# Statistics on two engines and begun with the weights, first projection by row pairs, x1 stored from ScalarE's queue

## The chip, the cores and the metric

The kernel runs on one core of a Trainium2 chip. The metric is the device time of one execution in microseconds (us), as a median of several runs. A profiled execution was taken beside them, with a record of every instruction and DMA.

## The reference

Input is x, an image of 512 x 512 positions with 128 channels, in fp32. Two layers follow each other, each as x = x + layer(gn(x)):

```
gn(v)    = (v - mean) / sqrt(var + 1e-5)           # 32 groups of 4 channels, over all positions
layer 0:   a = sigmoid((x@Wa1 + ba1) * (x@Wa2 + ba2))        # 128 -> 16 channels
           b = sigmoid((x@Wb1 + bb1) * (x@Wb2 + bb2))
           z = einsum('ikc,jkc->ijc', a, b)                  # 16 channels
           out = sigmoid(x@Wg + bg) * (layernorm(z)@Wz + bz)
layer 1:   h = (ln(x)@pi) * sigmoid(ln(x)@gi) * mask         # 128 channels, then
           two triangle products of 32 channels each, layernorm, output projection and gate
```

## The kernel before

`pair_layers` builds stages that follow each other behind a barrier of all engines. The weights' preparation (`prepare`), then:

1. `stage1_statistics` reads x once (134 MB) in 16 chunks of 8.4 MB, 128 positions x 128 channels on each of 128 partitions, into a double buffer. VectorE takes a bn_stats (count, mean, variance) of each of the 32 channel groups in every chunk (128 x 512 values each, L286), then aggregates them (L291). TensorE averages over partitions, and both small engines turn the moments into `gn_scale` and `gn_shift`.
2. `stage2_gates` is the first projection. It reads x again, a group of U = 4 image rows (1 MB) at a time, 128 groups. For every row TensorE transposes four 128 x 128 blocks into PSUM (`turn`, L385), ScalarE scales and rounds them to fp16 (`round_high`, L425), VectorE makes the fp16 rest (`rest`, L468). Then `product` (L395) multiplies high and low parts with the 32-wide weights, for m = 0 and m = 1, four rows side by side in the array's columns, 12 matmuls each m. ScalarE adds a bias to m = 0 (`open_first`, L430), VectorE multiplies it with m = 1 (`multiply`, L475), ScalarE takes the sigmoid (`sigmoid`, L436), and SP stores four groups together. The loop's body holds 8 groups and turns 15 times; the last 8 groups are written out.
3. `stage3_triangle` is layer 0's product over k, to z. It is not touched.
4. `stage4_layer0` makes x1, 16 rows a loop turn, 32 turns. For each row i TensorE does the z projection (L793), the gate projection (L795) and the four transposes of row i+4 (L785); ScalarE does the sigmoid (L821) and copies the transposed x (L817); VectorE mixes them (L854) and takes statistics of the sum (L845); GpSimd adds x (L888). The SP queue, per group of 4 rows: wait for the four sums (`added`), store x1 (L754), wait until x's tile is transposed, load x for the group 16 rows on (two DMAs, L745), wait for the z projection, load z (two DMAs, L749).
5. Stages 5 to 7 (mask, projection, triangle products and output of layer 1) are not touched. Stage 7 stores its output from ScalarE's queue (L1602) while SP loads.

The order of the work in each stage is written out by hand in each engine's program. An engine runs its instructions in this order, and each waits for semaphores: `turned`, `rounded`, `rest_ready`, `done` (products), `opened`, `gated`, `sig` in stage 2. A counter that is set ahead (`dve.sem_inc(gated, 2)`) says how many buffers are free at the start.

In stage 2 before, one step of TensorE is: turn rows 0 and 1 of group g+2, product m=0 of group g+1, turn rows 2 and 3, product m=1 of g+1. ScalarE: round rows 0 and 1 of g+2, open g+1, round rows 2 and 3, sigmoid g. VectorE: rest of rows 0 and 1 of g+2, multiply g, rest of rows 2 and 3. `p_ps` is doubled: both products wait for `gated >= g+1`, which multiply(g-2) gives.

Of the kernel before, what the change touches and what calls it, by code (L numbers as in the profile page):

```python
# [11 lines left out]
P = 128  # L12
BANK = 512
# [38 lines left out]
def prepare(nc, K, W):  # L52

    with ExitStack() as stack:
# [31 lines left out]
        with nc.Block() as block:  # L86
            @block.sync
            def _(sp):
                for dst, src in loads:
                    sp.dma_start(dst, src).then_inc(loaded, 16)  # L90
                sp.wait_ge(loaded, 16 * len(loads))
# [162 lines left out]
def stage1_statistics(nc, K, x, N):  # L254

    T = 128
    chunks = N * N // P // T
    x_v = x.rearrange("(p n t) c -> n p t c", p=P, t=T)
    with ExitStack() as stack:
        s = Scope(nc, stack, "s1")  # L260
        xt = s.sbuf("xt", [P, 2, T, P])
        stats = s.sbuf("stats", [P, 32, chunks, 6])
        mv = s.sbuf("mv", [P, 32, 2])
        square = s.sbuf("square", [P, 32])
# [3 lines left out]
        used, aggregated, wide_ready, moments_ready = s.sem("used"), s.sem("aggregated"), s.sem("wide_ready"), s.sem("moments_ready")  # L268
        with nc.Block() as block:
            norm_vector, norm_scalar = norm_from_moments(nc, s, block, K, moments, moments_ready)  # L270

            @block.sync
            def _(sp):
                with sp.Fori(0, chunks // 2) as r:
                    for u in range(2):
                        sp.wait_ge(used, r * 2 + (u + 1))
                        sp.dma_start(xt[:, u, :, :], x_v[bass.ds(r * 2 + u, 1)].rearrange("a p t c -> p (a t) c")).then_inc(loaded[u], 16)

            @block.vector
            def _(dve):  # L280
                dve.sem_inc(used, 2)
                with dve.Fori(0, chunks // 2) as r:
                    for u in range(2):
                        dve.wait_ge(loaded[u], r * 16 + 16)
                        for g in range(32):
# [3 lines left out]
                dve.wait_ge(used, chunks + 2)  # L289
                for g in range(32):  # L290
                    dve.bn_aggr(mv[:, g, :], stats[:, g, :, :].rearrange("p n s -> p (n s)")).then_inc(aggregated, 1)  # L291
                dve.wait_ge(aggregated, 32)
                dve.tensor_tensor(square[:], mv[:, :, 0], mv[:, :, 0], ALU.mult).then_inc(aggregated, 1)
                dve.tensor_copy(wide[:, 0, :, :], mv[:, :, 0:1].to_broadcast([P, 32, 4]))
                dve.wait_ge(aggregated, 33)
                dve.tensor_tensor(square[:], square[:], mv[:, :, 1], ALU.add).then_inc(aggregated, 1)
                dve.wait_ge(aggregated, 34)
                dve.tensor_copy(wide[:, 1, :, :], square[:].rearrange("p (g a) -> p g a", a=1).to_broadcast([P, 32, 4])).then_inc(wide_ready, 1)
# [10 lines left out]
            @block.scalar  # L309
            def _(act):  # L310
                norm_scalar(act)
# [9 lines left out]
def stage2_gates(nc, K, x, ab_d, N):  # L321
# [4 lines left out]
    CB, U, GROUPS = N // P, 4, 8  # L326
    REPS = N // (U * GROUPS)
    x_v = x.rearrange("(i p q) c -> p i q c", q=CB, p=P)
    ab_v = ab_d.rearrange("(g j) c k -> (j c) g k", j=U)
    with ExitStack() as stack:  # L330
        s = Scope(nc, stack, "s2")
        xt = s.sbuf("xt", [P, GROUPS, U, CB, P])
        high, low = s.sbuf("high", [P, 4, U, N], FP16), s.sbuf("low", [P, 4, U, N], FP16)
        first, gate = s.sbuf("first", [P, 2, N]), s.sbuf("gate", [P, 2, N])
        ab = s.sbuf("ab", [P, 2, 4, N])
# [6 lines left out]

        BODY = GROUPS * U

        @block_of(nc)
        def _(block):
            @block.sync
            def _(sp):
                def load(r, k):
                    sp.dma_start(xt[:, k, :, :, :], x_v[:, bass.ds(r * BODY + U * k, U)]).then_inc(loaded[k], 16)  # L350

                def store(r, half):
                    sp.wait_ge(sig, r * GROUPS + (4 * half + 4 + 2))
                    sp.dma_start(ab_v[:, bass.ds(r * GROUPS + 4 * half, 4), :], ab[:, half, :, :]).then_inc(stored[half], 16)
# [5 lines left out]
                with sp.Fori(0, REPS - 1) as r:  # L360
                    for k in range(GROUPS):
                        sp.wait_ge(turned, r * BODY + (U * k + U))
                        load(r + 1, k)
                        if k == 5:
                            store(r, 0)
                    store(r, 1)
                for half in range(2):
                    store(REPS - 1, half)
                for half in range(2):
                    sp.wait_ge(stored[half], REPS * 16 + 16)  # L370

            @block.tensor
            def _(pe):
                for m in range(2):
                    pe.matmul(p_ps[:, m, 0, 0:1], K.Wab4[:, m, :], K.gn_shift[:], start=True, stop=True).then_inc(shifted, 1)
                pe.wait_ge(folded, 2)
                pe.sem_inc(done, 8)

                def turn(r, g, j):

                    if j == 0:
                        pe.wait_ge(loaded[g % GROUPS], (r + g // GROUPS) * 16 + 16)
                    pe.wait_ge(rest_ready, r * BODY + (U * g + j + 1))
                    for q in range(CB):
                        last = pe.transpose(x_ps[:, j, q * P:(q + 1) * P], xt[:, g % GROUPS, j, q, :], K.ident[:])  # L385
                    last.then_inc(turned, 1)

                def product(r, g, m):
                    pe.wait_ge(rest_ready, r * BODY + (U * g + U + U))
                    pe.wait_ge(gated, r * GROUPS + (g + 1))  # L390
                    half = slice(32 * m, 32 * m + 32)
                    for weights, part, start, stop in ((K.Wab_high, high, True, False), (K.Wab_low, high, False, False),
                                                       (K.Wab_high, low, False, True)):
                        for j in range(U):
                            last = pe.matmul(p_ps[32 * j:32 * j + 32, g % 2, m, 0:N], weights[:, half], part[:, g % 4, j, :],  # L395
# [3 lines left out]
                def step(r, g, last=False):  # L399
                    for j in range(U):  # L400
                        if not (last and g + 2 >= GROUPS):
                            turn(r, g + 2, j)
                        if j % 2 == 1 and not (last and g + 1 >= GROUPS):
                            product(r, g + 1, j // 2)

                for g in range(2):
                    for j in range(U):
                        turn(0, g, j)
# [5 lines left out]
                for g in range(GROUPS):  # L414
                    step(REPS - 1, g, last=True)

            @block.scalar
            def _(act):
                act.sem_inc(sig, 2)

                def round_high(r, g, j):
                    act.wait_ge(turned, r * BODY + (U * g + j + 1))
                    if j == 0:
                        act.wait_ge(done, r * (2 * GROUPS) + (2 * g + 2))
                    act.activation(high[:, g % 4, j, :], x_ps[:, j, 0:N], ACT.Copy, scale=K.gn_scale[:]).then_inc(rounded, 1)  # L425

                def open_first(r, g):
                    act.wait_ge(done, r * (2 * GROUPS) + (2 * g + 1 + 8))
                    act.wait_ge(gated, r * GROUPS + (g + 1))
                    act.activation(first[:, g % 2, :], p_ps[:, g % 2, 0, 0:N], ACT.Identity, bias=bias[:, 0:1]).then_inc(opened, 1)  # L430

                def sigmoid(r, g):
                    act.wait_ge(gated, r * GROUPS + (g + 1 + 2))
                    if g % 4 == 0:
                        act.wait_ge(stored[g // 4], r * 16 + 16)
                    act.activation(ab[:, g // 4, g % 4, :], gate[:, g % 2, :], ACT.Sigmoid).then_inc(sig, 1)  # L436

                def step(r, g, last=False):
                    for j in range(U):
                        if not (last and g + 2 >= GROUPS):  # L440
                            round_high(r, g + 2, j)
                        if j == 1 and not (last and g + 1 >= GROUPS):
                            open_first(r, g + 1)
                    sigmoid(r, g)

                for g in range(2):
                    for j in range(U):
                        round_high(0, g, j)
                act.wait_ge(folded, 2)
                open_first(0, 0)  # L450
                with act.Fori(0, REPS - 1) as r:
                    for g in range(GROUPS):
                        step(r, g)
                for g in range(GROUPS):
# [1255 lines left out]
```

## Time and profile before

| | us |
|---|---|
| median of 3 runs | 5023.39 (5017.31 to 5030.55) |
| the profiled execution | 5046.03 |
| its span (first to last instruction) | 5044.3 |

| engine | busy us | share |
|---|---|---|
| TensorE | 4064.9 | 81% |
| VectorE | 4109.2 | 81% |
| ScalarE | 3366.2 | 67% |
| GpSimd | 2717.9 | 54% |

Shares are means over stages with different limits, so they are read by stage. "DMA share" is the mean busy share of the 16 DMA engines; where transfers overlap in an engine it can pass 1. SPq and ACTq are the queues of SyncE and ScalarE as they issue. "x4" behind an instruction says that four alike are merged in a row. An idle time in brackets stands before the instruction, with what ended it.

### The profile page before, as it was taken

The page shows a single profiled execution, that of the slowest core. Times are in us where ns is not written, and L with a number is a line of the kernel's source. Part 1 is how long each engine was busy: PE and PEld are TensorE (multiplying, and loading weights), DVE is VectorE, ACT ScalarE, POOL GpSimd, SP SyncE. Part 2 cuts the span into 40 slices and gives each one's busy share as a digit, 9 for nine tenths or more (in the row PEclk, how much of TensorE's full clock was granted, in tenths as well). Part 3 has the DMA queues.
Part 4 walks back from the last instruction along what each step waited for, and adds up shares of the span by engine and source line. Part 5 has one row for each costly group of instructions (what it writes and reads, how often), then busy time and mean ns, then how long its engine had stood idle before and what let it go on. Part 6 is the DMA issues. An engine that isn't in the chain of part 4 may idle for free. (4 is left out here: it accounts for less than half of the span.)

```text
span 5044.3 us, 90362 instructions
## 1 busy us (share of the span) xinstructions
PE 4064.9 (81%) x26438; PEld 2297.6 (46%) x26438; DVE 4109.2 (81%) x5835; ACT 3366.2 (67%) x4752; POOL 2717.9 (54%) x1426
## 2 busy tenths in 40 slices
PE   0004888893799999879999999989998886888888
PEld 0002555451455555545555555555553333444444
DVE  5888888688788888879999999867778887777777
ACT  0004999754677777658888888746666666888887
POOL 0000000093677777757777777743334435888887
PEclk9999999996899999989999999999999998999999
DMA  6996888653999999968888888776676757999999
GB/s 269 368 373 263 322 321 320 230 175 125 324 355 356 355 354 353 332 234 310 308 309 311 312 309 309 260 254 225 225 238 236 237 195 296 408 406 405 402 403 367
DMA packets 700450, 1532.72 MB, mean 304 GB/s; under 512 B 32800, under 2 KB 50656, under 8 KB 697952
## 3 DMA queue, kind: packets, MB, share of 16 engines
q1 hardware_dynamic: 632800, 1397.68, 78.3%
q10 hardware_dynamic: 67584, 134.23, 6.9%
q8 instruction: 34, 0.56, 0.0%
q14 instruction: 32, 0.26, 0.0%
HBM read 1009.59 MB, written 522.19 MB: 304 GB/s over the span
## 5 line engine op out<-in xcount | busy, mean ns | idle before, releaser
L1634 POOL TENSOR_TENSOR s_oT<-s_gated,s_x1t 128x1024 f32<-128x1024 f32 x256 | 689.6, 2699 | 223.5 <-DVE s_gated L1553 218.5
L888 POOL TENSOR_TENSOR s_x1T<-s_gz,s_xT 128x512 f32<-128x512 f32 x512 | 652.4, 1274 | 202.9 <-DVE s_gz L854 199.8
L1321 PE MATMUL s_y_ps<-s_ab 128*128 128x512 f16 x3072 | 698.0, 385 | 66.3 <-DVE s_ab L1391 64.7
L1026 POOL TENSOR_TENSOR s_low<-s_xc,s_high 128x1024 f16<-128x1024 f32 x256 | 547.8, 2140 | 265.0 <-ACT s_high L989 263.8
L795 PE MATMUL s_g_ps<-s_xT,s_Wg 128*128 128x512 f32 x1024 | 523.7, 593 | 0.0
L634 POOL MEMSET s_total<- 128x2048 f32 x1 | 1.8, 1810 | 960.4 <-POOLq L41 960.4
L854 DVE SCALAR_TENSOR_TENSOR s_gz<-s_z_ps,k_z_bias,s_g 128x512 f32<-128x512 f32 x512 | 384.1, 750 | 164.4 <-ACT s_g L821 162.1
L1321 PEld LDWEIGHTS s_y_ps<-s_ab 128*128 128x128 f16 x3072 | 301.4, 99 | 426.6 <-issue 94.9
L821 ACT ACTIVATE s_g<-s_g_ps,s_bg 128x512 f32<-128x512 f32 x512 | 352.0, 687 | 191.4 <-PE s_g_ps L795 191.4
L1553 DVE SCALAR_TENSOR_TENSOR s_gated<-s_p_ps,k_po_bias,s_gate 128x1024 f32<-128x1024 f32 x256 | 328.6, 1284 | 176.4 <-ACT s_gate L1590 147.7
L1295 POOL TENSOR_TENSOR s_at<-s_at,s_mask 128x1024 f32<-128x1024 f32 x64 | 164.2, 2566 | 502.2 <-DMA s_bt<-h_d 502.2
L468 DVE SCALAR_TENSOR_TENSOR s_low<-s_x_ps,k_gn_scale,s_high 128x512 f16<-128x512 f32 x512 | 359.6, 744 | 88.8 <-ACT s_high L425 88.3
L994 ACT ACTIVATE s_gate<-s_g_ps,k_gi_bias 128x1024 f32<-128x1024 f32 x256 | 284.9, 1113 | 200.3 <-PE s_g_ps L1165 199.8
L785 PEld LDWEIGHTS s_x_ps<-k_ident,s_xt 128*128 128x128 f32 x2048 | 247.5, 142 | 359.9 <-issue 205.3
L1590 ACT ACTIVATE s_gate<-s_g_ps,k_go_bias 128x1024 f32<-128x1024 f32 x256 | 285.8, 1116 | 147.6 <-PE s_g_ps L1499 134.2
L1097 DVE SCALAR_TENSOR_TENSOR s_h<-s_p_ps,k_pi_bias,s_gate 128x1024 f32<-128x1024 f32 x256 | 327.2, 1278 | 63.2 <-DMA h_d<-s_h 26.0
L1064 DVE BATCH_NORM_STATS2 s_stats<-s_x_ps 128x6 f32<-128x256 f32 x1024 | 363.0, 416 | 18.2 <-PE s_x_ps L1142 17.3
L286 DVE BATCH_NORM_STATS2 s_stats<-s_xt 128x512 f32 x512 | 305.5, 682 | 74.8 <-DMA s_xt<-in_x 74.8
L785 PE MATMUL s_x_ps<-k_ident,s_xt 128*128 128x128 f32 x2048 | 315.3, 277 | 54.8 <-DMA s_xt<-in_x 47.7
L845 DVE BATCH_NORM_STATS2 s_stats<-s_x1T 128x512 f32 (+1 forms) x512 | 349.5, 683 | 0.2 <-POOL s_x1T L888 0.2
L817 ACT ACTIVATE s_xT<-s_x_ps 128x512 f32<-128x512 f32 x512 | 302.7, 591 | 51.6 <-PE s_x_ps L785 50.2
L425 ACT ACTIVATE s_high<-s_x_ps,k_gn_scale 128x512 f16<-128x512 f32 x512 | 323.7, 686 | 13.0 <-PE s_x_ps L385 8.3
(215 smaller groups left out, 9695.3 us busy)
## 6 DMA issues: line engine op xcount, KB each, us to landing
s_xt<-in_x SPq DMA_DIRECT2D x128, 1024.0 KB, 6.9
s_xt<-in_x SPq DMA_DIRECT2D x256, 512.0 KB
x_d<-s_x1T SPq DMA_DIRECT2D x128, 1024.0 KB, 8.8
s_xt<-x_d SPq DMA_DIRECT2D x128, 1024.0 KB, 8.7
h_d<-s_h SPq DMA_DIRECT2D x128, 1024.0 KB, 6.4
s_x1t<-x_d SPq DMA_DIRECT2D x128, 1024.0 KB, 13.8
out<-s_ot ACTq DMA_DIRECT2D x128, 1024.0 KB, 9.3
s_mask_b<-mask_d SPq DMA_DIRECT2D x128, 512.0 KB, 4.3
```

Source lines behind the costliest of these rows:

```text
L468: dve.scalar_tensor_tensor(low[:, g % 4, j, :], x_ps[:, j, 0:N], K.gn_scale[:], high[:, g % 4, j, :], ALU.mult, ALU.subtract).then_inc(res ...
L785: last = pe.transpose(x_ps[:, i % 4, q * P:(q + 1) * P], xt[:, i // U, i % U, q, :], K.ident[:])
L795: pe.matmul(g_ps[:, i % 2, 0:N], Wg[:], xT[:, i % 8, :], start=True, stop=True).then_inc(g_prod, 1)
L821: act.activation(g[:, i % 2, :], g_ps[:, i % 2, 0:N], ACT.Sigmoid, bias=bg[:]).then_inc(sig, 1)
L845: dve.bn_stats(stats[:, bass.ds(r * ROWS + i, 1), :].rearrange("p a s -> p (a s)"), x1T[:, i // U, i % U, :]).then_inc(counted, 1)
L854: dve.scalar_tensor_tensor(gz[:, i % 4, :], z_ps[:, i % 2, 0:N], K.z_bias[:], g[:, i % 2, :], ALU.add, ALU.mult).then_inc(mixed, 1)
L888: pool.tensor_tensor(x1T[:, i // U, i % U, :], gz[:, i % 4, :], xT[:, i % 8, :], ALU.add).then_inc(added, 1)
L1026: pool.tensor_tensor(low[:, n % 4, :, :], xc[:, n % 4, :, :], high[:, n % 4, :, :], ALU.subtract).then_inc(rest_ready, 1)
L1064: last = dve.bn_stats(stats[:, row // 16 % 2, row % 16, a, :], x_ps[:, row % 2, 2 * a * P:(2 * a + 2) * P].rearrange("p (e c) -> p c e", c=P))
L1321: last = pe.matmul(y_ps[:, ib, 0:N], ab[:, u % 2, 0, a, kb, ib * P:(ib + 1) * P], ab[:, u % 2, 1, b, kb, :], start=m == 0, stop=m == len(t ...
L1553: dve.scalar_tensor_tensor(gated[:, n % 4, :, :], p_ps[:], K.po_bias[:], gate[:, n % 2, :, :], ALU.add, ALU.mult).then_inc(mixed, 1)
L1634: pool.tensor_tensor(oT[:, n % 4, :, :], gated[:, n % 4, :, :], x1t[:, n // 2, 2 * (n % 2):2 * (n % 2) + 2, :], ALU.add).then_inc(added, 1)
```

## The change

**Statistics.** VectorE keeps 24 of the 32 channel groups; ScalarE takes 8, with two activations a group (Identity and Square), each of which adds up its output in `accum_out`. The first two chunks are issued on the SP queue before the 38 weight loads, in `prepare`. A buffer is loaded again when both engines have read it.

**First projection.** Rounding and rest work on pairs of rows, 1024 elements. `x_ps` has three slots of two PSUM banks each (it had four of one), and `p_ps` one bank for each m (it had two). ScalarE rounds three groups ahead. A loop turn holds 6 groups, 20 turns, and 8 groups are written out. SP reloads six groups, then stores three groups at a time.

**Layer 0's stage.** ScalarE issues the store of x1, at the third row of the next group; SP only loads. The first of the 32 loop turns is written out.

```
 # stage1_statistics
+        def load_ahead(sp):
+            for u in range(2):
+                load(sp, 0, u)
+        prepare(nc, K, W, load_ahead)        # load_ahead(sp) runs ahead of the weights' loads
...
             def _(sp):
+                with sp.Fori(0, chunks // 2 - 1) as r:
                     for u in range(2):
                         sp.wait_ge(used, r * 2 + (u + 1))
+                        sp.wait_ge(summed, r * 2 + (u + 1))
+                        load(sp, r + 1, u)
...
             def _(act):
+                def chunk(r, u):
+                    act.wait_ge(loaded[u], r * 16 + 16)
+                    if not isinstance(r, int) or r or u:
+                        act.wait_ge(summed, r * 2 + u)
+                    for g in range(BY_ACT):
+                        for m, func in enumerate((ACT.Identity, ACT.Square)):
+                            last = act.activation(junk[:, 2 * g + m, :].rearrange("p (t c) -> p t c", c=4),
+                                                  xt[:, u, :, 4 * (BY_DVE + g):4 * (BY_DVE + g) + 4], func,
+                                                  accum_out=sums[:, m, g, bass.ds(r * 2 + u, 1)])
+                    last.then_inc(summed, 1)
...
             def _(dve):     # after 24 bn_aggr
+                dve.wait_ge(summed, chunks)
+                dve.tensor_reduce(total[:], sums[:], AX.X, ALU.add).then_inc(reduced, 1)
+                dve.wait_ge(reduced, 1)
+                dve.tensor_scalar(total[:], total[:], 1.0 / (4 * T * chunks), None, ALU.mult).then_inc(reduced, 1)
+                dve.wait_ge(reduced, 2)
+                for m in range(2):
+                    last = dve.tensor_copy(wide[:, m, BY_DVE:32, :], ...)

 # stage2_gates
-    CB, U, GROUPS = N // P, 4, 8
+    CB, U, GROUPS, SLOTS = N // P, 4, 6, 3
-        x_ps = s.psum("x_ps", [P, U, BANK])
-        p_ps = s.psum("p_ps", [P, 2, 2, BANK])
+        x_ps = s.psum("x_ps", [P, SLOTS, 2, BANK])
+        p_ps = s.psum("p_ps", [P, 2, BANK])
...
             def _(sp):
                 with sp.Fori(0, REPS - 1) as r:
                     for k in range(GROUPS):
+                        reload(r, k)
+                    for half in range(2):
+                        store(r, half)
...
             def _(pe):
+                def turn(r, g, h):
+                    k, n = g % GROUPS, (2 * g + h) % SLOTS
+                    if h == 0:
+                        pe.wait_ge(loaded[k], (r + g // GROUPS) * 16 + 16)
+                    pe.wait_ge(rest_ready, r * PAIRS + (2 * g + h + 1))
+                    for j in range(2):
+                        for q in range(CB):
+                            last = pe.transpose(x_ps[:, n, j, q * P:(q + 1) * P], xt[:, k, 2 * h + j, q, :], K.ident[:])
                     last.then_inc(turned, 1)
                 def product(r, g, m):
-                    pe.wait_ge(gated, r * GROUPS + (g + 1))
+                    pe.wait_ge(rest_ready, r * PAIRS + (2 * g + 2 + SLOTS))
+                    if m == 0:
+                        pe.wait_ge(opened, r * GROUPS + (g + 1))
+                    else:
+                        pe.wait_ge(gated, r * GROUPS + (g + 2))
...
+                def step(r, g, end=None):
+                    for h in range(2):
+                        if end is None or g + 2 < end:
+                            turn(r, g + 2, h)
+                        if end is None or g + 1 < end:
+                            product(r, g + 1, h)
...
             def _(act):
+                def step(r, g, end=None):
                     sigmoid(r, g)
+                    if end is None or g + 3 < end:
+                        round_high(r, g + 3, 0)
+                    if end is None or g + 2 < end:
+                        open_first(r, g + 2)
+                    if end is None or g + 3 < end:
+                        round_high(r, g + 3, 1)
...
             def _(dve):
+                dve.sem_inc(rest_ready, SLOTS)
                 dve.sem_inc(gated, 2)
+                def step(r, g, end=None):
+                    if end is None or g + 2 < end:
+                        rest(r, g + 2, 0)
+                    multiply(r, g)
+                    if end is None or g + 2 < end:
+                        rest(r, g + 2, 1)

 # stage4_layer0
             def _(sp):
-                def group(r, n, last=False):
-                    sp.wait_ge(added, r * ROWS + (U * n + U + 8))
-                    sp.dma_start(x1_d[...], x1T[:, n, :, :]).then_inc(stored[n], 16)
-                    if not last:
+                def group(r, n):
+                    sp.wait_ge(turned, r * ROWS + (U * n + U))
+                    load_x(r + 1, n)
+                    sp.wait_ge(z_prod, r * ROWS + (U * n + U))
+                    load_z(r + 1, n)
...
             def _(act):
+                def store(r, n):
+                    act.wait_ge(added, r * ROWS + (U * n + U + 8))
+                    act.dma_start(x1_d[...], x1T[:, n, :, :]).then_inc(stored[n], 16)
+                def step(r, i, first=False, last=False):
                     act.wait_ge(g_prod, r * ROWS + (i + 1))
                     act.activation(g[:, i % 2, :], g_ps[:, i % 2, 0:N], ACT.Sigmoid, bias=bg[:]).then_inc(sig, 1)
                     if not (last and i + 4 >= ROWS):
                         keep(r, i + 4)
+                    if i % U == 2 and i > U:
+                        store(r, i // U - 1)
+                    elif i % U == 2 and not first:
+                        store(r - 1, GROUPS - 1)
```

## Rows read from the trace of the kernel before

**Rows 1.** Timeline, statistics pass: start us, length us, engine, line, operation, idle time before.

```profile
37.58 1.00 SPq L277 DMA_DIRECT2D s_xt<-in_x  x2
...
62.89 19.09 DVE L286 BATCH_NORM_STATS2 s_stats<-s_xt 128x512 f32 x32 [26.50 <-DMA s_xt<-in_x]
...
83.31 19.09 DVE L286 BATCH_NORM_STATS2 s_stats<-s_xt 128x512 f32 x32 [1.33 <-DMA s_xt<-in_x]
107.59 19.09 DVE L286 BATCH_NORM_STATS2 s_stats<-s_xt 128x512 f32 x32 [5.18 <-DMA s_xt<-in_x]
...
397.57 19.09 DVE L286 BATCH_NORM_STATS2 s_stats<-s_xt 128x512 f32 x32 [0.89 <-DMA s_xt<-in_x]
416.69 14.44 DVE L291 BATCH_NORM_AGGREGATE s_mv<-s_stats 128x2 f32<-128x96 f32 x32
```

**Rows 2.** Timeline, the weights' preparation: its first and its last VectorE instruction.

```profile
23.55 0.36 DVE L170 COPY k_Wab<-w_Wab 128x128 f32<-128x128 f32 x2 [23.55 <-DMA k_bias<-in_bb]
...
36.09 0.29 DVE L221 TENSOR_TENSOR k_Wgo<-w_wide,k_Wgo 128x128 f16<-128x128 f32 x1
```

**Rows 3.** Busy us of each engine by stretch; granted clock, DMA share and GB/s last.

```profile
447.00:955.00 508.00, 457.79 (x5028) 273.51 (x5024) 425.74 (x628) 488.82 (x783) 0.00 (x0) 1.00 0.89 321
1300.00:2130.00 830.00, 781.71 (x3499) 462.80 (x3498) 674.88 (x1001) 600.75 (x1000) 636.87 (x500) 1.00 1.04 354
4240.00:5000.00 760.00, 664.50 (x4910) 330.44 (x4912) 593.09 (x703) 618.47 (x936) 631.59 (x234) 1.00 1.05 405
```

**Rows 4.** Timeline, first projection: one turn of the chain in the steady part.

```profile
600.18 0.40 PE L395 MATMUL s_p_ps<-s_high,k_Wab_high 128*32 128x512 f16 x4
...
600.94 1.09 PE L385 MATMUL s_x_ps<-k_ident,s_xt 128*128 128x128 f32 x8
601.06 0.69 ACT L430 ACTIVATE s_first<-s_p_ps,s_bias 128x512 f32<-128x512 f32 x1
601.65 1.26 ACT L425 ACTIVATE s_high<-s_x_ps,k_gn_scale 128x512 f16<-128x512 f32 x2
601.75 0.74 DVE L475 SCALAR_TENSOR_TENSOR s_gate<-s_p_ps,s_bias,s_first 128x512 f32<-128x512 f32 x1
...
602.40 1.40 DVE L468 SCALAR_TENSOR_TENSOR s_low<-s_x_ps,k_gn_scale,s_high 128x512 f16<-128x512 f32 x2
...
603.93 0.40 PE L395 MATMUL s_p_ps<-s_high,k_Wab_high 128*32 128x512 f16 x4
```

**Rows 5.** Groups of the page: count, busy us, mean ns of one, idle before.

```profile
L994 ACT ACTIVATE s_gate<-s_g_ps,k_gi_bias 128x1024 f32<-128x1024 f32 x256 | 284.9, 1113 | 200.3 <-PE s_g_ps L1165 199.8
L1553 DVE SCALAR_TENSOR_TENSOR s_gated<-s_p_ps,k_po_bias,s_gate 128x1024 f32<-128x1024 f32 x256 | 328.6, 1284 | 176.4 <-ACT s_gate L1590 147.7
```

**Rows 6.** Groups by line, first microseconds to 1000: a table load.

```profile
L425 ACT ACT_TABLE_LOAD x15 | 19.2, 1283 | 1.4 <-PE s_x_ps L385 0.6
```

**Rows 7.** Timeline: first and last instruction of the first projection.

```profile
440.75 5.70 PE L385 MATMUL s_x_ps<-k_ident,s_xt 128*128 128x128 f32 x32 [4.45 <-DMA s_xt<-in_x]
...
961.06 0.63 ACT L436 ACTIVATE s_ab<-s_gate 128x512 f32<-128x512 f32 x1 [0.36 <-DVE s_gate L475]
```

**Rows 8.** Waits, 1285 to 2145: who waited for whom, total us, times, longest.

```profile
PE s_x_ps L785 <- DMA s_xt<-in_x: 47.7, 116, 0.9
...
SPq L754 <- POOL s_x1T L888: 353.0, 128, 11.6
```

**Rows 9.** Layer 0's stage: GpSimd's sums (shortest/median/longest ns, first to last start), SP's stores.

```profile
L888 POOL TENSOR_TENSOR s_x1T<-s_gz,s_xT x512: 1264/1274/1286, 1292.2 to 2138.7; 128x512 f32<-128x512 f32 x171
...
1298.26 0.42 SPq L754 DMA_DIRECT2D x_d<-s_x1T  x1
...
1304.18 0.42 SPq L754 DMA_DIRECT2D x_d<-s_x1T  x1
```

**Rows 10.** Two lines of the kernel: a DMA issue on ScalarE's queue, and transposes.

```profile
L1602 ACTq DMA_DIRECT2D out<-s_ot x128: 378/378/453, 4218.3 to 5039.0; - x128
...
L785 PE MATMUL s_x_ps<-k_ident,s_xt x2048: 272/273/474, 1284.8 to 2131.7; 128*128 128x128 f32 x187
```

More of the change, by code:

```diff
@@ L310, in _ @@
             def _(act):
+                def chunk(r, u):
[8 more added lines that the diff above has]
+                    last.then_inc(summed, 1)
+                for u in range(2):
+                    chunk(0, u)
+                with act.Fori(1, chunks // 2) as r:
+                    for u in range(2):
+                        chunk(r, u)
                 norm_scalar(act)
@@ L394, in product @@
                         for j in range(U):
[L395 removed]
+                            last = pe.matmul(p_ps[32 * j:32 * j + 32, m, 0:N], weights[:, half], part[:, g % GROUPS, j, :],
                                              start=start, stop=stop)
                     last.then_inc(done, 1)
[L399 to L404, printed above, removed]
+                def step(r, g, end=None):
[4 more added lines that the diff above has]
+                            product(r, g + 1, h)
                 for g in range(2):
[L407 to L408 removed]
+                    for h in range(2):
+                        turn(0, g, h)
                 for m in range(2):
@@ L413, in _ @@
                         step(r, g)
-                for g in range(GROUPS):
-                    step(REPS - 1, g, last=True)
+                for g in range(TAIL):
+                    step(REPS - 1, g, TAIL)
             @block.scalar
@@ L432, in sigmoid @@
                 def sigmoid(r, g):
+                    k = g % GROUPS
                     act.wait_ge(gated, r * GROUPS + (g + 1 + 2))
[L434 to L443, printed above, removed]
-                    sigmoid(r, g)
+                    if k % 3 == 0:
+                        act.wait_ge(stored[k // 3], (r + g // GROUPS) * 16 + 16)
@@ L476, in multiply @@
                                              ALU.add, ALU.mult).then_inc(gated, 1)
-                def step(r, g, last=False):
-                    for j in range(U):
-                        if not (last and g + 2 >= GROUPS):
-                            rest(r, g + 2, j)
-                        if j == 1:
-                            multiply(r, g)
+                def step(r, g, end=None):
[4 more added lines that the diff above has]
+                        rest(r, g + 2, 1)
@@ L490, in _ @@
                         step(r, g)
-                for g in range(GROUPS):
-                    step(REPS - 1, g, last=True)
+                for g in range(TAIL):
+                    step(REPS - 1, g, TAIL)
 def stage3_triangle(nc, K, ab_d, z_d, N):
@@ L767, in _ @@
                         group(r, n)
-                for n in range(GROUPS):
-                    group(N // ROWS - 1, n, last=True)
                 for n in range(GROUPS):
@@ L828, in _ @@
                     keep(0, i)
-                with act.Fori(0, N // ROWS - 1) as r:
+                for i in range(ROWS):
+                    step(0, i, first=True)
+                with act.Fori(1, N // ROWS - 1) as r:
                     for i in range(ROWS):
```

143 lines of the change are left out of this document (73 added, 70 removed).

## The prediction

> **What bounds the kernel now.** I read the busy time by stretches first, then in each stretch that the change touches the chain that repeats. Three stretches are touched, with three different limits. The statistics pass (37 to 434 us) lives on its loads: VectorE sits idle 1.33 and 5.18 us before two of the chunks shown, each time for a load, and 32 bn_stats of a chunk take 19.09 us [rows 1]. The first projection (441 to 962 us) has ScalarE busy 489 of 508 us and TensorE 458 of 508, at full granted clock [rows 3]. Which of them sets the pace is told only by the chain of one row group (four image rows), below. Layer 0's output stage (1292 to 2140 us) has TensorE at 782 of 830 us and GpSimd at 637, but its DMA share is 1.04 throughout at 354 GB/s [rows 3], TensorE waits for x loads [rows 8], and the queue of SyncE stands 353 us waiting for GpSimd's sums [rows 8]. Everything else is left as it is.
>
> **Statistics pass.** The two first 8.4 MB chunks are now issued ahead of the 45 small weight loads, on the same SP queue. Nothing of the weights can land before them: before, two chunks issued at 37.58 were there at 62.89 and 83.31 [rows 1], so 45.7 us after issue. Issued at 0.9 they are there at 46.6. The preparation began at 23.55, as soon as the last weight had landed, and its last VectorE instruction is at 36.09 [rows 2]; moved to 47.5 it ends at 60.3, and bn_stats can start at about 62, as before (62.89). So the early load hides nothing of the first chunk; what it wins is that the second is there too. From then on VectorE has 24 groups a chunk, 24 x 0.597 = 14.3 us (19.09/32 = 0.597), and ScalarE takes 8 groups with two activations each. The trace has no activation with accum_out. The nearest is the sigmoid from SBUF on 128x512, 0.63 us [rows 7], so 16 make 10.1 us; from above they may cost 1.27 each, 20.4 a chunk, before they cost anything, since the load takes that long. Below that price neither they nor a table load of 1.28 us in each loop turn shows. One load alone took 25.4 us (issued when the first chunk had been read, at 62.89 + 19.09 = 82.0, there at 107.59 less a hop); one that was queued behind another took 20.4 [rows 1]. Before, a load was issued 19.1 us after its predecessor's predecessor had arrived, so every second one started late, and chunks came 22.3 us apart ((397.57-62.89)/15). Now it is issued after 14.3 us, always with another in flight: 20.4 apart. Chunk 2 is issued at 76.4 and there at 101.8, chunk 15 at 101.8 + 13 x 20.4 = 367.0, done at 381.3. Before, that was 416.7: 35.4 less. The aggregation has 24 instead of 32 instructions of 0.451 (14.44/32), 3.6 less; a reduce, a scaling and two small copies are added, about 1.2 by their neighbours' 0.2 to 0.3 each with a hop. **Together 38 less.** The other end, if chunks still come 22.3 apart: 391.7 + 14.3 = 406.0, so 13 less in all.
>
> **First projection.** What is removed: four 512-wide roundings and four 512-wide rests a group become two of each on 1024. Rows with that width are 1.113 us for ScalarE from PSUM and 1.284 for VectorE [rows 5], against 0.69 and 0.74 for 512 [rows 4]: started back to back with the overlap of about 0.1 that the openings and roundings at 601.06 and 601.65 show, ScalarE has 4 x 0.59 - 2 x 1.01 = 0.3 us less a group, VectorE also some 0.3. The body begins with the sigmoid, so I expect one table load a turn (20 turns) in place of two (15 turns, [rows 6] has one of the two): 13 us less on ScalarE.
>
> What decides is the chain. First the old one, as a test of the method. In step order TensorE runs product m=0 (600.18), then transposes (600.94); ScalarE's first opens at 601.06, two roundings start at 601.65, their two rests at 602.40 and take 1.40, and the next product starts at 603.93: 0.88 + 0.59 + 0.75 + 1.40 + 0.13 = 3.75, which is the distance of the two products [rows 4]. With the table loads and the loop turns it is 521/128 = 4.07 in the mean (the stage runs from 440.75 to 961.69, [rows 7]).
>
> The new order closes a tighter ring. The two product tiles in PSUM are no longer doubled, so product(g, m=1) waits for gated >= g+2, which is multiply(g-1). VectorE reaches multiply(g-1) only behind rest(g+1, 0), in its program order; that rest needs round_high(g+1, 0), and that needs turn(g+1, 0), all eight transposes of a pair. But turn(g+1, 0) is the first item of the same TensorE step whose last item is product(g, 1), and the next step's first turn is queued behind it. So one group costs at least: 8 transposes 1.09, hop 0.05, rounding 1.11, hop 0.05, rest 1.19 before the multiply can follow (1.284 less the 0.09 by which multiply and rest overlap at 601.75 and 602.40), multiply 0.74, hop to TensorE 0.13, product until the next turn 0.76. **Sum 5.12 us**, with the terms from [rows 4, 5]. The hops are those of the old chain (602.40 after a rounding's end at 602.34; 603.93 after 603.80). A second ring, product 0, turn 1, rounding 1, rest 1, product 0, has 0.76 + 1.09 + 0.05 + 1.11 + 0.05 + 1.28 + 0.13 = 4.47 and stays inside the first. TensorE stands still about 1.4 us in each group, ahead of product 1; the table load at the loop's head (1.28) falls into ScalarE's idle time of 1.3 to 2 us after the sigmoid's input and costs about nothing, as do the loads (one 1 MB load in 5.1 us against 4.07 now) and the stores, that SP now issues after six reloads in place of between them. The stage: 5.6 to the first product, 127 x 5.12 = 650, 4.5 to drain, 660 against 521: **139 more.** From both sides: 5.0 (the two hops of 0.05 at nothing) gives 124 more; 5.3 (no overlap on VectorE, 0.3 us a turn of loop cost) gives 162.
>
> **x1 stored from ScalarE's queue.** Now SP waits for the sums before each store, and the x and z loads stand behind it; moved, they are issued as soon as their own tiles are free, some four rows earlier. Each store puts 0.38 us on ScalarE's sequencer [rows 10], once in four rows, plus a wait for `added`, behind which the next sigmoid is queued (VectorE's mix waits for that). The sum it waits for is three rows old, so the wait is met; the issue falls where ScalarE idles for TensorE anyway (0.3 us a row). Pace now: (2138.7-1292.2)/511 x 4 = 6.63 us per four rows [rows 9]. With all buffers full at the start it was 5.92 (1298.26 to 1304.18, [rows 9]), TensorE's own pace. To hold 6.0 the engines must move 354 x 6.63 / 6.0 = 391 GB/s. One queue gave 354 here at a share of 1.04; the last stage, whose stores go by ScalarE's queue, had 405 at 1.05 [rows 3]. That is the nearest row for two queues, so I take 6.15: 0.48 x 128 = **61 less**. Ends: no gain at 354 GB/s; 0.71 x 128 = 91 less at 5.92; and, if each issue were fully exposed, 0.38 x 128 = 49 more.
> A rule speaks against this gain. The Trainium skill, "DMA: Bandwidth & Descriptors", section "Issuing engines are not separate DMA queues", says that DMAs issued by any engine run on the same 16 DMA engines, and that several issuers save only issue time. By that rule this term would be 0, not 61. The 354 against 405 GB/s speaks against the rule here, though the two stages differ in more than the queue.
>
> **Sum.** The profiled execution took 5046.0 (span 5044.3): 5046 - 38 + 139 - 61 = 5086. It lay 22.6 above the median of the runs, 5023.4, so the forecast is 5086 - 22.6 = 5063, rounded 5064.
>
> **Rivals.**
> A: the store's move gives nothing because the 16 engines are full (share 1.04 in every stretch); the stage keeps 6.63. 5064 + 61 = 5125. Against it the 405 GB/s. 18 in 100.
> B, on the other side: the projection speeds up to TensorE's own pace, because the rounding runs three groups ahead and ScalarE (489 of 508 us busy) was the limit. Price: 2 x (0.76 + 1.09) = 3.70 a group, 10 + 127 x 3.70 = 480, 41 less; 5046 - 38 - 41 - 61 - 22.6 = 4883. For it speaks the busy share; against it that product 1 waits for the multiply of the same step. With the other two gains (99 us) the whole becomes faster than before if the group takes under 4.07 + 99/128 = 4.84. 10 in 100.
> C: TensorE, idle 1.4 us in each group, falls to its lower clock. A transpose is 273 ns at the high and 474 at the low level [rows 10]; turn and product, 1.85 of the ring, would take about 3.2: 6.5 a group, 173 more, 5237. Against it: the stretch from 4240 kept 1.00 with TensorE idle 12% of the time. 5 in 100.
> D: both gains at their far ends (40 and 91) with a ring of 5.0: 5046 - 40 - 91 + 124 - 22.6 = 5016, no difference to speak of. 12 in 100.
>
> **How the numbers follow.** The forecast has 55 in 100; its own range is 5035 to 5095. Changes under 0.3% (15 us) can't be told from none here, the runs before lie within 13 us. A, C and the forecast are slower but for 3 in 100 of the forecast's near end; D is the same for the most part: slower 0.75, same 0.13, faster 0.12. The range 5012 to 5135 leaves B below, C above.
>
> **What would show it.** First bn_stats still near 62 us, 14.3 us a chunk, chunks 20 us apart. In the projection: products m=1 at a distance of 5.1 us, TensorE's longest wait there for the multiply (s_gate), a busy share of TensorE near 75%, ScalarE near 65%, granted clock 1.00, the stage 660 us long. In layer 0's stage four rows in 6.0 to 6.3 us, DMA above 370 GB/s, no wait for x. Wrong if the products come closer than 4.8 us, or if four rows still take 6.6.

## The result and the profile after

| | before | after |
|---|---|---|
| median of 20 runs each, us | 5039.9 (5017.3 to 5074.1) | 5076.1 (5070.1 to 5079.2) |
| span of the profiled execution, us | 5044.3 | 5076.9 |

The change makes the kernel slower by 0.7%: the ratio is 1.0067, with an interval from 1.0051 to 1.0082. Forecast was slower, 5064 us. The spans, taken apart by stage:

| stage | before, us | after, us | difference | forecast |
|---|---|---|---|---|
| up to the first transposes of the projection | 0 to 440.75 | 0 to 412.44 | -28.3 | -38 |
| first projection | 520.9 | 655.8 | +134.9 | +139 |
| from there to the first sum of layer 0's stage | 330.5 | 329.5 | -1.0 | 0 |
| layer 0's stage, first to last sum | 846.5 | 771.6 | -74.9 | -61 |
| everything after | 2905.6 | 2907.6 | +2.0 | 0 |
| whole | 5044.3 | 5076.9 | +32.6 | +40 |

Timeline of the changed kernel, first projection: the chain of one group, that answers to [rows 4].

```profile
700.62 0.40 PE L445 MATMUL s_p_ps<-s_high,k_Wab_high 128*32 128x512 f16 x4 [1.48 <-DVE s_gate L532]
...
701.38 1.09 PE L432 MATMUL s_x_ps<-k_ident,s_xt 128*128 128x128 f32 x8
...
702.60 1.11 ACT L476 ACTIVATE s_high<-s_x_ps,k_gn_scale 128x1024 f16<-128x1024 f32 x1
...
703.74 1.28 DVE L525 SCALAR_TENSOR_TENSOR s_low<-s_x_ps,k_gn_scale,s_high 128x1024 f16<-128x1024 f32 x1 [1.99 <-ACT s_high L476]
...
704.95 0.74 DVE L532 SCALAR_TENSOR_TENSOR s_gate<-s_p_ps,s_bias,s_first 128x512 f32<-128x512 f32 x1
...
705.74 0.40 PE L445 MATMUL s_p_ps<-s_high,k_Wab_high 128*32 128x512 f16 x4 [1.48 <-DVE s_gate L532]
```

The product m=1 ends the ring, the turn follows at 0.76, and the next product m=1 starts 705.74 - 700.62 = 5.12 us later, having stood 1.48 us for `s_gate`, the multiply. The next turn of the ring (705.74 to 710.86) is as long. The busy row and the waits of the projection and the busy row of layer 0's stage, beside [rows 3] and [rows 8]:

```profile
440.00:1050.00 610.00, 434.29 (x4777) 259.22 (x4770) 373.76 (x358) 434.15 (x496) 0.00 (x0) 1.00 0.74 253
```

```profile
PE s_p_ps L445 <- DVE s_gate L532: 183.1, 124, 1.6
ACT s_high L476 <- PE s_x_ps L432: 142.8, 105, 1.4
```

```profile
1500.00:2100.00 600.00, 600.00 (x2781) 375.35 (x2780) 536.58 (x795) 466.66 (x795) 505.64 (x398) 1.00 1.05 390
```

```profile
L950 POOL TENSOR_TENSOR s_x1T<-s_gz,s_xT x512: 1263/1272/1282, 1397.7 to 2169.3; 128x512 f32<-128x512 f32 x171
```

No engine bounds the projection any more: TensorE and ScalarE are both busy 71% of it, and the DMA engines move 253 GB/s where they had 321. The clock stayed at its upper level, 1.00. In layer 0's stage TensorE has no gap left; four rows take (2169.3-1397.7)/511 x 4 = 6.04 us against 6.63 [rows 9]. That is TensorE's own pace, and it could be read from the kernel before, where the stage begins and nothing is waited for: 1.51 us from one row's transposes to the next one's, 6.04 for four.

```profile
1290.41 0.60 PE L785 MATMUL s_x_ps<-k_ident,s_xt 128*128 128x128 f32 x4
...
1291.92 0.60 PE L785 MATMUL s_x_ps<-k_ident,s_xt 128*128 128x128 f32 x4
```

The statistics pass, the SP queue first, then VectorE (it answers to [rows 1] and [rows 2]):

```profile
0.83 0.89 SPq L276 DMA_DIRECT2D s_xt<-in_x  x2
...
5.96 34.58 SPq L91 DMA_DIRECT2D w_gi<-in_gi_w  x1
40.59 4.85 SPq L91 DMA_DIRECT2D w_po<-in_po_w  x1
45.48 0.43 SPq L91 DMA_DIRECT2D w_go<-in_go_w  x1
```

```profile
63.97 0.36 DVE L171 COPY k_Wab<-w_Wab 128x128 f32<-128x128 f32 x2 [63.97 <-DMA k_bias<-in_bb]
...
77.98 28.57 DVE L300 BATCH_NORM_STATS2 s_stats<-s_xt 128x512 f32 x48 [1.18 <-PEq L41]
...
118.73 14.35 DVE L300 BATCH_NORM_STATS2 s_stats<-s_xt 128x512 f32 x24 [12.18 <-DMA s_xt<-in_x]
138.09 14.33 DVE L300 BATCH_NORM_STATS2 s_stats<-s_xt 128x512 f32 x24 [5.00 <-DMA s_xt<-in_x]
...
390.65 10.87 DVE L305 BATCH_NORM_AGGREGATE s_mv<-s_stats 128x2 f32<-128x96 f32 x24
```

SP itself stood: the issue of one weight load took 34.58 us and of the next 4.85, until the 16.8 MB ahead had been moved (45.5 us, my 46.6). The other 36 loads (there are 45, as the prediction has it, not 38) were issued only then, over 17 us, so the weights landed at 63.97, not at 47.5, and the statistics began at 77.98, not at 62.

### The profile page after: what moved, and what is told of

Read it like the earlier page. It is cut to its first block and busy times, and to the rows that moved or that the text cites. A ratio compares the mean times of both kernels' runs of the same rounds, so it can differ in the third digit from the quotient of the medians.

```text
span 5076.9 us, 89620 instructions
## 1 busy us (share of the span) xinstructions
PE 4038.9 (80%) x26438; PEld 2306.8 (45%) x26438; DVE 3996.1 (79%) x5447; ACT 3480.1 (69%) x4999; POOL 2714.1 (53%) x1426
## 5 line engine op out<-in xcount | busy, mean ns | idle before, releaser
L525 DVE SCALAR_TENSOR_TENSOR s_low<-s_x_ps,k_gn_scale,s_high 128x1024 f16<-128x1024 f32 x256 | 327.3, 1279 | 257.6 <-ACT s_high L476 257.6
L476 ACT ACTIVATE s_high<-s_x_ps,k_gn_scale 128x1024 f16<-128x1024 f32 x256 | 285.1, 1114 | 155.5 <-PE s_x_ps L432 153.4
L1204 PE MATMUL s_x_ps<-k_ident,s_xt 128*128 128x128 f32 x2048 | 290.3, 280 | 35.8 <-DVE s_stats L1126 18.3
L1152 DVE TENSOR_TENSOR s_xc<-s_xt,s_r_ps 128x1024 f32<-128x1024 f32 x256 | 310.3, 1212 | 8.0 <-PE s_r_ps L1219 4.4
L837 PE MATMUL s_x_ps<-k_ident,s_xt 128*128 128x128 f32 x2048 | 308.5, 274 | 7.0 <-DMA s_xt<-in_x 7.0
```

What stands on the lines that cost most here:

```text
L837: last = pe.transpose(x_ps[:, i % 4, q * P:(q + 1) * P], xt[:, i // U, i % U, q, :], K.ident[:])
```

## The experiments

Each is the changed kernel with one part or order different. The one with turns and products in blocks changes the order on three engines at once, and the last puts several changes together. Each stage time is read from one profiled execution.

### The old projection back

```
-    CB, U, GROUPS, SLOTS = N // P, 4, 6, 3
+    CB, U, GROUPS = N // P, 4, 8         # and all of stage2_gates as before the change
```

> The changed kernel with the first projection as it was before; statistics and x1 store stay changed. Theory (the new ring alone makes the change slow, the three parts add up): the projection takes 521 us again instead of 656, the whole about 5076 - 135 = 4941, some 2% below the kernel before, the statistics 28 and layer 0's stage 75 shorter as in the changed kernel. Rival (the stages influence each other, for example by the clock or by what the stage after has to wait for): layer 0's stage or the triangle stage between changes by more than 10 us against the changed kernel.

Measured: 4940.9 us against 5044.1, ratio 0.9795 (0.9743 to 0.9847), span 4942.1. The projection takes 520.9 us (411.3 to 932.1), layer 0's stage 771.6. The triangle stage between takes 330.3, as before. The three parts add up, and the projection alone turns a gain of 2% into a loss. No stage leaned on another.

### VectorE multiplies first

```
                 def step(r, g, end=None):       # VectorE
-                    if end is None or g + 2 < end:
-                        rest(r, g + 2, 0)
                     multiply(r, g)
+                    if end is None or g + 2 < end:
+                        rest(r, g + 2, 0)
```

> The changed kernel with one line moved: VectorE multiplies group g before the rest of group g+2's first pair, no longer after it. Theory (the ring turn 0, rounding 0, rest 0, multiply, product 1 sets 5.12 us a group): it is cut, and the second ring (product 0, turn 1, rounding 1, rest 1, product 0) is left with 4.47; the stage 10 + 127 x 4.47 = 578, 78 less, the whole about 4998. Rival (the wide instructions or the single product tile as such cost the time, not the order): still 5.0 to 5.1 us a group, whole 5076. Second rival (ScalarE's table load at the loop's head is now exposed): 4.47 in the body and about 1 us more once in six groups, whole about 5018.

Measured: 4989.7 us, ratio 0.9887 (0.9836 to 0.9937). The projection takes 567.9 us (411.8 to 979.7), 88 less than in the changed kernel. Waits in it, with who waits, for whom, the total, the times and the longest:

```profile
DVE s_low L525 <- ACT s_high L476: 155.9, 145, 1.3
...
PE s_p_ps L445 <- DVE s_low L525: 95.9, 124, 0.9
```

```profile
601.53 0.40 PE L445 MATMUL s_p_ps<-s_high,k_Wab_high 128*32 128x512 f16 x4 [0.74 <-DVE s_low L525]
...
605.99 0.40 PE L445 MATMUL s_p_ps<-s_high,k_Wab_high 128*32 128x512 f16 x4 [0.82 <-DVE s_low L525]
```

TensorE no longer waits for the multiply but for the rest, as the second ring says, and its products m=0 are 605.99 - 601.53 = 4.46 us apart, where that ring was forecast at 4.47. The wide instructions, the single product tile and the three slots are all still there, so the order of two instructions on VectorE made 88 of the 135 us. 127 such groups are 566 us, so in a stage of 567.9 that holds all 20 table loads there is no room for 1 us more once in six groups, and the second rival falls too. The 47 us that remain over the old projection come with the second ring, which the next experiment takes away.

### Turns and products of a step in blocks

```
-    TensorE: turn 0, product 0, turn 1, product 1
+    TensorE: turn 0, turn 1, product 0, product 1
-    ScalarE: sigmoid g, round g+3 pair 0, open g+2, round g+3 pair 1
+    ScalarE: open g, round g+2 pair 0, sigmoid g, round g+2 pair 1
-    VectorE: rest g+2 pair 0, multiply g, rest g+2 pair 1
+    VectorE: multiply g, rest g+2 pair 0, rest g+2 pair 1
```

> The changed kernel's tiles and wide instructions, in another order: TensorE turns both pairs of g+2 and then multiplies both m of g+1; ScalarE opens g, rounds pair 0 of g+2, sigmoid g, rounds pair 1; VectorE multiplies g, then both rests. Theory (only the order made the rings): no ring through one group is left but TensorE's own work, 2 x 0.76 + 2 x 1.02 to 1.09 = 3.6 to 3.7 a group, the stage 470 to 480 us, the whole 4892 to 4902, below the kernel before. Rival (ScalarE, about 3.2 us a group and a table load in each turn of six, becomes the bound): 3.9 to 4.1 a group, the stage as before (521), whole 4941.

Measured: 4937.0 us, ratio 0.9786 (0.9736 to 0.9836); the projection 517.1 us (412.1 to 929.2). ScalarE's timeline over one group and then over the loop's head:

```profile
603.71 0.64 ACT L490 ACTIVATE s_ab<-s_gate 128x512 f32<-128x512 f32 x1 [0.43 <-DVE s_gate L528]
...
607.35 0.64 ACT L490 ACTIVATE s_ab<-s_gate 128x512 f32<-128x512 f32 x1 [0.42 <-DVE s_gate L528]
607.89 1.10 ACT L477 ACTIVATE s_high<-s_x_ps,k_gn_scale 128x1024 f16<-128x1024 f32 x1
...
611.00 0.63 ACT L490 ACTIVATE s_ab<-s_gate 128x512 f32<-128x512 f32 x1 [0.43 <-DVE s_gate L528]
...
612.65 1.28 ACT L483 ACT_TABLE_LOAD   x1
613.94 0.69 ACT L483 ACTIVATE s_first<-s_p_ps,s_bias 128x512 f32<-128x512 f32 x1
614.53 1.11 ACT L477 ACTIVATE s_high<-s_x_ps,k_gn_scale 128x1024 f16<-128x1024 f32 x1
615.65 1.28 ACT L490 ACT_TABLE_LOAD   x1
616.95 0.63 ACT L490 ACTIVATE s_ab<-s_gate 128x512 f32<-128x512 f32 x1
```

Inside a turn of the loop the sigmoids start at 603.71, 607.35 and 611.00: 3.64 us apart, the theory's number. Its reason does not hold, though: TensorE still stands 0.25 us in each group for the rest (`s_low`), so 3.64 is not its own work alone, and the last experiment shows it at 3.30. Across the loop's head it is the rival's: two table loads, 616.95 - 611.00 = 5.95 us for that group on an engine that has only 0.4 us to spare in the others, and (5 x 3.64 + 5.95)/6 = 4.03 in the mean. Both were half right: the two long rings are gone, and the second table load is the next thing that costs.

### The x chunks behind the weights' loads

```
             def _(sp):                       # prepare
-                load_ahead(sp)
                 for dst, src in loads:
                     sp.dma_start(dst, src).then_inc(loaded, 16)
+                load_ahead(sp)
```

> The changed kernel with the two x chunks issued behind the weights' loads instead of ahead of them. Theory (SP stood 34.6 and 4.9 us at two weight loads behind 16.8 MB, so the preparation ended at 77 instead of 37): weights there at 23.6, preparation done at 37.5, chunk 0 issued at 22.5 and there at 48, chunk 2 issued at 62.4 and there at 88, chunk 15 at 88 + 13 x 19.8 = 345 instead of 376: about 31 us less, whole 5045. Rival (the preparation hides behind the loads anyway, since chunks limit the pass): less than 10 us less.

Measured: 5049.5 us against 5044.1 for the kernel before, ratio 1.0001 (0.9976 to 1.0026). The span is 5040.6, 36 less than the changed kernel's; the medians differ by 27, for the profiled execution was the shortest of the ten. VectorE starts at 48.28 and the last chunk comes at 346.13:

```profile
48.28 14.34 DVE L300 BATCH_NORM_STATS2 s_stats<-s_xt 128x512 f32 x24 [11.83 <-DMA s_xt<-in_x]
68.63 14.34 DVE L300 BATCH_NORM_STATS2 s_stats<-s_xt 128x512 f32 x24 [6.02 <-DMA s_xt<-in_x]
...
346.13 14.34 DVE L300 BATCH_NORM_STATS2 s_stats<-s_xt 128x512 f32 x24 [4.99 <-DMA s_xt<-in_x]
```

The first transposes are at 382.2 in place of 412.4: some 30 us that the position of two DMA issues in a queue had cost. (Six profiled kernels have the changed kernel's statistics pass: five had them at 411.3 to 412.4 and one at 419.4, so the last few us are open.)

### One chunk ahead, one behind

```
             def _(sp):                       # prepare
-                load_ahead(sp)                # chunks 0 and 1
+                load_ahead(sp)                # chunk 0
                 for dst, src in loads: ...
+                load_behind(sp)               # chunk 1
```

> The changed kernel with one x chunk ahead of the weights' loads and the second behind them. Theory (SP stands at a weight load because the two chunks fill what its queue holds, not because of the weight loads' count): with 8.4 MB ahead SP stands much less than 39 us or not at all, the weights land about when the chunk has, 24 to 27 us, the preparation is done at 38 to 41, bn_stats start there instead of at 78. Chunk 1 is there at about 45. The pass then ends about 35 us earlier than in the changed kernel. Rival (any x chunk ahead holds the weights up by the same stall): SP stands some 15 to 20 us, the preparation ends at 50 to 60.

One run, 5056.7 us, span 5054.4. VectorE starts at 56.97, and the first transposes come at 394.6, 18 us earlier than in the changed kernel and not 35. SP stands 17.23 us, at the ninth weight load:

```profile
5.93 17.23 SPq L91 DMA_DIRECT2D w_po<-in_po_w  x1
23.20 0.45 SPq L91 DMA_DIRECT2D w_go<-in_go_w  x1
```

It stands until about 23 us with 8.4 MB ahead and until 45 with 16.8, that is until the x bytes are moved, after seven or eight small loads in either case. The rival holds. The count of the chunks ahead sets how long SP stands, not whether. That the queue holds only so much is my reading of it. In both kernels the issue that first stands is the tenth DMA on the queue, with 16.8 MB ahead as with 8.4, so a limit in bytes doesn't fit; what it counts, the runs don't tell.

### One queue, loads early

```
             def _(sp):                       # layer 0's stage; ScalarE no longer stores
                     sp.wait_ge(turned, ...); load_x(r + 1, n)
                     sp.wait_ge(z_prod, ...); load_z(r + 1, n)
+                    store(r, n - 1)           # waits for added, of the group before
```

> The changed kernel with the x1 store back on SP's queue, but one group late, behind the loads, so that its wait is met when SP comes to it. The loads are issued as early as with the store on ScalarE's queue. Theory A (a second queue lets the 16 DMA engines move more): one queue still gives about 354 GB/s, four rows take 6.4 to 6.6 us, the stage is 50 to 75 us longer than in the changed kernel. Rival B (only the late issue of the loads behind the waiting store cost time): four rows in 6.04, as in the changed kernel, at 390 GB/s.

### Two queues, loads late

```
             def _(sp):                       # layer 0's stage; ScalarE stores
-                    sp.wait_ge(turned, r * ROWS + (U * n + U))
+                    sp.wait_ge(added, r * ROWS + (U * n + U + 8))
                     load_x(r + 1, n)
```

> The changed kernel (x1 stored from ScalarE's queue), but SP again waits for the four sums (in place of the transposes, which they imply) before it loads x, as the kernel before did; only the queue of the store differs from it. The run with one queue and early loads gave 6.37 us for four rows at 372 GB/s, between the two theories, with GpSimd waiting for stores. Theory A (the second queue is most of it): four rows in 6.04 to 6.2 us, although the loads are issued late. Rival B (early loads are most of it, the queue only the rest): 6.3 to 6.6.

One run each: 5120.8 us with one queue, 5097.6 with two. The sums of GpSimd (from the first start to the last, over 511 intervals) of the two, and the busy row of each between 1500 and 2100 us, DMA share and GB/s last. One queue, loads early:

```profile
L958 POOL TENSOR_TENSOR s_x1T<-s_gz,s_xT x512: 1261/1273/1297, 1396.3 to 2209.6; 128x512 f32<-128x512 f32 x171
...
  DMA x_d<-s_x1T: 121.5, 87
```

```profile
1500.00:2100.00 600.00, 583.94 (x2646) 351.26 (x2645) 513.63 (x756) 448.57 (x756) 469.46 (x379) 1.00 1.04 372
```

Two queues, loads late:

```profile
L950 POOL TENSOR_TENSOR s_x1T<-s_gz,s_xT x512: 1263/1271/1282, 1405.8 to 2191.0; 128x512 f32<-128x512 f32 x171
```

```profile
1500.00:2100.00 600.00, 596.98 (x2732) 365.26 (x2731) 526.78 (x780) 460.84 (x782) 496.01 (x391) 1.00 1.05 384
```

| us per four rows (GB/s) | store on SP's queue | store on ScalarE's queue |
|---|---|---|
| loads late | 6.63 (354), the kernel before | 6.15 (384) |
| loads early | 6.37 (372) | 6.04 (390), the changed kernel |

The queue alone gives 0.48 us per four rows, early loads alone 0.26, both 0.59. With one queue and early loads GpSimd waits 121.5 us for stores to land; SP's wait merely changed hands. With two queues and early loads TensorE's own pace is reached, and the rest is cut off by it.

Moving the store also moved it in time. In the kernel before it was issued 0.6 us ahead of the x loads (1654.47 and 1655.08); on ScalarE's queue with late loads it went out over 2 us behind them (1657.40 and 1655.15). A store behind the loads is also what the one queue with early loads has, and at 6.37 that is still slower than two queues with late loads at 6.15, so the order alone does not explain the gain.

How firm the cells are differs. The changed kernel's stage took 771.6 or 771.7 us in all seven profiled kernels that have it. The other three cells are one execution each: stages of 846.5, 813.3 and 785.2 us, 28 to 61 apart. Over 20 runs the whole kernel before spread by 57 us and the changed one by 9, and nothing here shows which stage carries that spread. So the gain of both together is safe, and the split into 0.48 and 0.26 is rough.

### All of it in one kernel

```
     x chunks behind the weights' loads; TensorE and VectorE in blocks as above
-    ScalarE: open g, round g+2 pair 0, sigmoid g, round g+2 pair 1
+    ScalarE: sigmoid g, open g+1, round g+3 pair 0, round g+3 pair 1
```

> Everything that the runs pointed to in one kernel: x chunks behind the weights' loads, statistics on two engines, the projection in the new order but with ScalarE's step begun by the sigmoid (sigmoid g, open g+1, both roundings of g+3), x1 stored from ScalarE's queue. The new order alone ran at 3.64 us a group inside a loop turn and lost 5.9 us in the group with the two table loads (open first, sigmoid second). Theory (the loads were two because the turn began with a function of another table): one table load a turn, which the 0.4 us that ScalarE idles in each group hides for the most part; 3.64 to 3.8 a group, the stage 475 to 490 us, the whole 4865 to 4880 in the profile, 3.4% below the kernel before. Rival (loads of x at 3.64 us a group need 360 GB/s on one queue and fall behind): 3.8 to 4.0 a group, TensorE waiting for x, whole about 4900.

Measured: 4849.0 us against 5042.1, ratio 0.9608 (0.9580 to 0.9637). The projection is 448.1 us (387.4 to 835.5), and it and the whole come out below the forecast ranges. Its busy row, and TensorE over one group:

```profile
400.00:840.00 440.00, 417.47 (x5011) 280.82 (x5008) 394.58 (x377) 426.26 (x524) 0.77 (x1) 1.00 1.01 367
```

```profile
601.05 0.40 PE L445 MATMUL s_p_ps<-s_high,k_Wab_high 128*32 128x512 f16 x4
...
602.46 1.97 PE L432 MATMUL s_x_ps<-k_ident,s_xt 128*128 128x128 f32 x16
...
604.35 0.40 PE L445 MATMUL s_p_ps<-s_high,k_Wab_high 128*32 128x512 f16 x4
```

Three engines are at 90 to 97% and the DMA share at 1.01. One table load is left in a turn, of 1.28 us, and the groups between are about 3.1 to 3.3 us long. TensorE's own work in a group is 604.35 - 601.05 = 3.30 us, not the 3.6 to 3.7 that the expectations took from turns and products that alternate. The 20 table loads saved make at most 20 x 1.28 = 26 of the 69 us between this stage and the one with the turns in blocks; the shorter groups are the larger part. The kernel changes several things at once, so which of them shortened the groups is not shown.

## Why the prediction was right

- **The ring of the projection.** Its terms came out nearly one by one: in the turn shown 0.76 from product to turn, 1.22 to the rounding (1.14 forecast), 1.14 to the rest (1.16), 1.21 to the multiply (1.19), 0.79 to the product (0.87). The sum is 5.12 as forecast, to the hundredth by some luck: the hop from transposes to rounding is 0.12 to 0.13 and not 0.05 (also in the next group, where there is no table load: turn at 706.50, rounding at 707.71), and the last hop is 0.05 and not 0.13. The stage took 655.8 against 660; 127 x 5.12 is 650, so the first product and the drain took 5.6 us and not 10. That the ring was the cause, and not a figure that happened to fit, is shown by cutting it: the second ring, forecast at 4.47, came up in its place. The test of the method on the old chain (3.75) was weaker than it looked: over the same time ScalarE's own four pieces of work follow each other with 0.12 us idle (its openings start at 601.06 and 604.81), so 3.75 could not tell the chain from rival B's busy engine. The experiment with the multiply first does.
- **The table load** fell from 30 to 20 in all and was hidden, as said, by ScalarE's idle time ahead of the sigmoid.
- **The statistics pass** is where a step failed. "Nothing of the weights can land before them" was right, but I put their issue at SP's usual pace and only their landing later. The issues themselves stood 39 us, so the start came 16 us later than "at about 62", and chunk 2 came at 118.73 for 101.8. One term went the other way: chunks came (376.27-118.73)/13 = 19.8 us apart, not 20.4 (the last bn_stats ended at 390.65 against 381.3). The end of the pass cost what was said (24 aggregations in 10.87, reduce, scaling and copies about 1.0). 16 activations with their accumulator reads took 9.9 us (the last chunk's, 376.31 to 386.21), against 10.1. Net -28 for -38.
- **The x1 store** was mis-sized: 6.04 us for four rows, not 6.15, so 75 for 61. The 6.15 was a choice between 5.92 and 6.63 and not worked out. And 5.92 was no pace of TensorE's but the distance of two store issues; its own rows say 6.04, and the stage reached that, at the 390 GB/s that go with it. The mechanism holds, two queues moved 384 GB/s where one moved 354 with the same loads and waits. The rule against it (the Trainium skill, "DMA: Bandwidth & Descriptors", "Issuing engines are not separate DMA queues": several issuers save issue time only) doesn't hold in this stage, and the measurement decides. What comes nearest to what it names, loads that SP issues earlier, is the smaller part, 0.26 of the 0.59.
- **The level.** I took the profiled execution to be 22.6 us above the median, from 3 runs; over 20 runs the median of before is 5039.9. The difference of the medians is 36 us, the forecast's was 40. Of the 12 us between 5064 and 5076, 16 are this and -4 the sum.
- **Luck.** The three terms were off by +10, -4 and -14 us, which largely cancel and add up to -8. The direction did not need this: +135 against -28 and -75 is slower by itself.
- **The signs named beforehand.** The distance of 5.1, the longest wait, the clock, the chunks 20 us apart, four rows within 6.0 to 6.3 at over 370 GB/s and no wait for x came true. The first bn_stats near 62 did not, and the busy shares were 71% and 71% where 75 and 65 had been named.

## What to carry to other kernels

When tiles are made wider and buffers fewer, write down for each engine what stands ahead of the instruction that frees a buffer, and follow it round to the same item of the next step; the length of that ring, from rows of the old trace, was the new pace here, whatever the busy shares said. Read an engine's own pace from its own rows where it waits for nothing, and in the order that it will have. A step that frees a tile goes first in its engine's order. Don't issue large transfers ahead of small ones that something waits for: they hold up not only the landing but the issuing engine. And if a stage has its DMA engines full with loads and stores in one queue, try the stores in another.

## What was not expected of the hardware

- SP's issue of a 64 KB load took 34.6 us behind 16.8 MB in the same queue; behind 8.4 MB a 32 KB load took 17.2. Each was the tenth DMA on the queue.
- One queue carried 354 GB/s of loads and stores together at a share of 1.04, and 372 when the loads were issued early; two carried 384 to 390 at 1.05. The share does not tell how much room is left.
- A read of the accumulator (0.186 us) follows each activation with `accum_out`, but overlaps with its neighbours: activations with their reads start 0.61 us apart, about what the activation alone lasts.
- A loop turn that begins with the bias or the rounding loads a table for it and then another for the sigmoid: 40 loads in 20 turns (30 in 15 in the kernel before), and 5.95 us for the group in which both fall instead of 3.64. Behind the sigmoid the same functions need no load, and where the sigmoid comes first a turn has one: 20.
